# Wide attention of a fused two-layer transformer kernel: the query's scale moved into its evacuation, three-operand norms, the value projection ahead of the transposes, GpSimd's row sends two per step, and unrolled code

## The reference

```python
def _L1_xattn_ref(x, context, Wq, Wk, Wv, Wo, bo):     # 8 heads of 64
    scale = DIM_HEAD ** (-0.5)                          # 1/8
    q, k, v = heads(x @ Wq), heads(context @ Wk), heads(context @ Wv)
    attn = softmax(einsum('bhnd,bhmd->bhnm', q, k) * scale)
    return merge(einsum('bhnm,bhmd->bhnd', attn, v)) @ Wo + bo
x = x + _L1_xattn_ref(_layernorm(x), ctx_1024, ...)
x = x + _L1_ffn_ref(_layernorm(x), ...)                 # router: top 2 of 8 experts
```

## Time and profile before

| what | value |
|---|---|
| three runs | 1889.76, 1894.3, 1899.87 us, median 1894.3 |
| the profiled execution | 1891.22 us, its span 1889.4 us |
| busy share of the span | PE 79%, DVE 71%, ACT 62%, POOL 42% |
| wide attention: first to last group's exponentials | from 1144.9 to 1564.6 us of the span |
| its time for one step, mean of 64 | about 6.6 us |

### The profile page before, as it was taken

How to read it: one execution, slowest core, us unless ns; L and a number is a source line. 1 busy time by engine, 2 the same in 40 slices (tenths; PEclk the granted TensorE clock), 3 DMA queues, 4 the chain that set the end, 5 groups by cost and what they waited for, 6 DMA issues and landing times. The chain is left out here.

```text
span 1889.4 us, 62815 instructions
## 1 busy us (share of the span) xinstructions
PE 1485.4 (79%) x22193; PEld 1104.1 (58%) x22194; DVE 1343.5 (71%) x3761; ACT 1175.7 (62%) x2992; POOL 793.7 (42%) x836
## 2 busy tenths in 40 slices
PE   3999999838999889984329968888888885799990
PEld 2666666516666666663218845666666664678780
DVE  4888877648888888874536646788877875566675
ACT  2766666615555545544319957988877982677770
POOL 1000000033333333313755543456677766776661
PEclk9999999959999999996559977999999996899995
DMA  2222121001001001100122220011111101223228
GB/s 83 64 61 69 59 62 50 26 17 35 24 31 36 27 28 35 36 20 19 44 72 70 71 73 13 24 35 41 33 47 36 32 30 53 71 86 107 74 72 268
DMA packets 119875, 100.92 MB, mean 53 GB/s; under 512 B 18355, under 2 KB 111030, under 8 KB 119632
## 3 DMA queue, kind: packets, MB, share of 16 engines
q1 hardware_dynamic: 97712, 67.62, 12.3%
q0 software_dynamic: 12928, 25.60, 3.9%
q10 hardware_dynamic: 8992, 4.47, 0.8%
HBM read 43.30 MB, written 32.96 MB: 40 GB/s over the span
## 5 line engine op out<-in xcount | busy, mean ns | idle before, releaser
L2643 POOL DMA_INDIRECT e_back<-e_out_rows,e_G x142 | 151.6, 1067 | 72.0 <-issue 49.0
L1604 ACT ACTIVATE w_weights<-w_pS,w_ng 128x77 f32<-128x77 f32 x512 | 158.0, 340 | 25.9 <-DVE w_ng L1702 25.8
L580 ACT ACTIVATE m_PT<-m_pS 128x1024 f32<-128x1024 f32 x128 | 130.5, 1020 | 61.6 <-PE m_pS L450 59.8
L580 ACT ACTIVATE a_PT<-a_pS 77x1024 f32<-77x1024 f32 x128 | 130.6, 1020 | 48.4 <-PE a_pS L450 47.5
L731 DVE TENSOR_REDUCE m_mx<-m_pM 128x8 f32<-128x1024 f32 x128 | 155.4, 1214 | 3.1 <-PE m_pM L421 3.0
L1212 POOL DMA_INDIRECT e_rows<-re_R,re_index x128 | 129.2, 1009 | 62.6 <-issue 38.0
L2664 DVE TENSOR_TENSOR e_gl<-e_g,e_gh 128x512 f16<-128x512 f32 x142 | 98.3, 692 | 58.8 <-ACT e_g L2619 53.6
L851 POOL TENSOR_SCALAR a_var<-a_aggr 128x4 f32<-128x4 f32 x16 | 3.1, 194 | 291.4 <-DVE a_aggr L655 291.4
L1824 POOL TENSOR_TENSOR w_weights<-w_weights,w_rec 128x616 f32<-128x616 f32 x64 | 78.0, 1219 | 105.0 <-DVE w_rec L1706 104.7
L2616 ACT ACTIVATE e_gh<-e_pU 128x512 f16<-128x512 f32 x142 | 84.8, 598 | 46.9 <-PE e_pU L135 46.9
L1604 ACT ACTIVATION_READ_ACCUMULATOR w_weights<-w_pS,w_ng 128x1 f32 x512 | 113.7, 222 | 0.0
(11 more groups left out here) (401 smaller groups left out, 5661.1 us busy)
## 6 DMA issues: line engine op xcount, KB each, us to landing
e_G<-e_rows SPq DMA_DIRECT2D x106, 132.0 KB, 2.3
e_B<-e_back SPq DMA_DIRECT2D x16, 512.0 KB, 6.9
X<-in_x SPq DMA_DIRECT2D x16, 256.0 KB, 3.0
Qs<-a_qh SPq DMA_DIRECT2D x128, 32.0 KB
Qs<-m_qh SPq DMA_DIRECT2D x128, 32.0 KB
Ks<-m_kh SPq DMA_DIRECT2D x32, 128.0 KB
YW<-e_back SPq DMA_DIRECT2D x16, 256.0 KB, 3.1
w_stage<-in_late SPq DMA_DIRECT2D x16, 256.0 KB
```

Of the source, the lines that this page charges most:

```text
L580: act.activation(PT[:NK, b % 2, 8 * half:8 * half + 8, :], pS[:NK, :, :], ACT.Exp, scale=float(1.0 / np.sqrt(HD))).then_inc(exp_done, 1)
L1604: ac = act.activation(weights[:, b % 2, n, :], pS[:, n // HB, n % HB, :KC], ACT.Exp, bias=ng[:, b % 2, n:n + 1], scale=float(WD) ** -0.5, ...
L2643: pool.indirect_dma_start(out=back, out_offset=bass.IndirectOffsetOnAxis(ap=G[:, r, s, D:D + 1].bitcast(I32), axis=0), in_=out_rows[:, r, ...
```

## The change

All of it is in wide attention and in the router's `norm`:

- The query's parts hold -Q/8: ACT's copy gets scale -0.125, and DVE's low part becomes a `scalar_tensor_tensor`. The scores come out as -s/8, so the minimum over them is the exponentials' bias itself. The second DVE instruction of `take_max` and its semaphore go; the exponential's scale is -1.
- Both norms become `scalar_tensor_tensor` with three operands: the row, the mean as per-partition scalar, and the inverse deviation as a broadcast tensor.
- PE projects the values ahead of the transposes of the weights, and ACT copies them ahead of the weights.
- The sends go two per step in every step (in the last group three): of a pair's 16, four in the even group (b = 2, 3), eight in the odd one, four in the even group after it (b = 0, 1).
- POOL's `share` comes ahead of `roots`; `split_late` becomes `late_high` at b = 0 and `late_low` at b = 2.
- The loop is gone: all 16 groups are written out.

```diff
+Q_SCALE = -0.125
 ...
     def norm(self, dve, g):
         ...
-            dve.tensor_scalar(self.R[...], self.S[...], self.aggr[:, b, 0:1], self.rstd[:, b:b + 1], ALU.subtract,
-                              ALU.mult).then_inc(self.rows, 1)
+            dve.scalar_tensor_tensor(self.R[...], self.S[...], self.aggr[:, b, 0:1],
+                                     self.rstd[:, b:b + 1].rearrange("p (o n) -> p o n", o=1).to_broadcast([P, 1, D]),
+                                     ALU.subtract, ALU.mult).then_inc(self.rows, 1)
 ...
-            far, first, count = (4, 4 + 3 * b, 3) if g[1] % 2 else (3, 2 * b - 4, 2 if b > 1 else 0)
+            if g[0] is None and g[1] == NG - 1:
+                far, first, count = 4, 4 + 3 * b, 3
+            elif g[1] % 2:
+                far, first, count = 4, 4 + 2 * b, 2
+            else:
+                far, first, count = (3, 2 * b - 4, 2) if b > 1 else (5, 12 + 2 * b, 2)
 ...
         def walk(engine, begin, step, finish):
             begin()
-            groups(engine, lambda g, p, nxt, nxt2: [step(g, p, b, nxt, nxt2) for b in range(GB)], 4)
+            straight(engine, lambda g, p, nxt, nxt2: [step(g, p, b, nxt, nxt2) for b in range(GB)])
 ...
                     project("k", shift(g, 1), b)
+                project_values(g, b, nxt2)
                 if one:
                     turn_weights(*one)
-                project_values(g, b, nxt2)
 ...
-                    act.activation(Qh[:, p, b, :], pP[:, :TG], ACT.Copy).then_inc(hi_made, 1)
+                    act.activation(Qh[:, p, b, :], pP[:, :TG], ACT.Copy, scale=Q_SCALE).then_inc(hi_made, 1)
 ...
-                                        bias=ng[:, b % 2, n:n + 1], scale=float(WD) ** -0.5,
+                                        bias=ng[:, b % 2, n:n + 1], scale=-1.0,
 ...
+                keep_values(g, b)
                 if one:
                     keep_weights(*one)
-                keep_values(g, b)
 ...
-                    dve.tensor_tensor(Ql[:, p, b, :], pP[:, :TG], Qh[:, p, b, :], ALU.subtract).then_inc(evac, 1)
+                    dve.scalar_tensor_tensor(Ql[:, p, b, :], pP[:, :TG], Q_SCALE, Qh[:, p, b, :], ALU.mult,
+                                             ALU.subtract).then_inc(evac, 1)
 ...
-                dve.tensor_reduce(out=mx[:], in_=pS[:]..., op=ALU.max, axis=AX.X).then_inc(m_max, 1)
-                dve.wait_ge(m_max, lin(g, GB, b + 1))
-                dve.tensor_scalar(ng[:, b % 2], mx[:], -float(WD) ** -0.5, None, ALU.mult).then_inc(neg, 1)
+                dve.tensor_reduce(out=ng[:, b % 2], in_=pS[:]..., op=ALU.min, axis=AX.X).then_inc(neg, 1)
 ...
+                if one:
+                    share(*one)
                 if b == 3 and made:
                     route.roots(pool, made)
-                if one:
-                    share(*one)
 ...
                     route.send(pool, away, first, count)
+                if b == 0:
+                    late_high(g)
                 if b == 2:
-                    split_late(g)
+                    late_low(g)
```

More of the change, by code:

```diff
@@ L1104, in norm @@
         for b in range(GB):
-            dve.tensor_scalar(self.R[:, g[1] % 4, b:b + 1, 0, 0:D], self.S[:, bass.ds(lin(g, GB, b), 1), :],
-                              self.aggr[:, b, 0:1], self.rstd[:, b:b + 1], ALU.subtract,
-                              ALU.mult).then_inc(self.rows, 1)
+            dve.scalar_tensor_tensor(self.R[:, g[1] % 4, b:b + 1, 0, 0:D], self.S[:, bass.ds(lin(g, GB, b), 1), :],
+                                     self.aggr[:, b, 0:1],
+                                     self.rstd[:, b:b + 1].rearrange("p (o n) -> p o n", o=1).to_broadcast([P, 1, D]),
+                                     ALU.subtract, ALU.mult).then_inc(self.rows, 1)
     def lo(self, dve, g, bank, part):
@@ L1382, in wide_attention @@
         V = sb("V", [P, GB, WH_, WD], F32)
-        mx, ng = sb("mx", [P, WH_], F32), sb("ng", [P, 2, WH_], F32)
+        ng = sb("ng", [P, 2, WH_], F32)
         weights, sums, rec = sb("weights", [P, 2, WH_, KC], F32), sb("sums", [P, 2, WH_], F32), sb("rec", [P, 2, WH_], F32)
@@ L1396, in wide_attention @@
         v_ready, v_kept = sem("v_ready"), sem("v_kept")
-        s_ready, m_max, neg, exp_done = sem("s_ready"), sem("m_max"), sem("neg"), sem("exp_done")
+        s_ready, neg, exp_done = sem("s_ready"), sem("neg"), sem("exp_done")
         rec_done, shared, w_turned, w_kept = sem("rec_done"), sem("shared"), sem("w_turned"), sem("w_kept")
@@ L1682, in norm_rows @@
                 for b in range(start, start + count):
-                    dve.tensor_scalar(xn[:, b:b + 1, :], X[:, bass.ds(lin(g, GB, b), 1), :], aggr[:, b, 0:1],
-                                      rstd[:, b:b + 1], ALU.subtract, ALU.mult).then_inc(x_norm, 1)
+                    dve.scalar_tensor_tensor(xn[:, b:b + 1, :], X[:, bass.ds(lin(g, GB, b), 1), :], aggr[:, b, 0:1],
+                                             rstd[:, b:b + 1].rearrange("p (o n) -> p o n", o=1).to_broadcast([P, 1, D]),
+                                             ALU.subtract, ALU.mult).then_inc(x_norm, 1)
             def part(what, g, p, b):
@@ L1698, in take_max @@
                 dve.wait_ge(s_ready, lin(g, GB, b + 1))
-                dve.tensor_reduce(out=mx[:], in_=pS[:].rearrange("p o k t -> p (o k) t")[:, :, :KC], op=ALU.max,
-                                  axis=AX.X).then_inc(m_max, 1)
-                dve.wait_ge(m_max, lin(g, GB, b + 1))
-                dve.tensor_scalar(ng[:, b % 2], mx[:], -float(WD) ** -0.5, None, ALU.mult).then_inc(neg, 1)
+                dve.tensor_reduce(out=ng[:, b % 2], in_=pS[:].rearrange("p o k t -> p (o k) t")[:, :, :KC], op=ALU.min,
+                                  axis=AX.X).then_inc(neg, 1)
             def invert(g, b):
@@ L1810, in rows, with late_high @@
                 pool.tensor_tensor(rstd[:], var[:], c["mhalf"][:, 0:GB], ALU.pow).then_inc(ln_rstd, 1)
-            def split_late(g):
+            def late_high(g):
                 cols = bass.ds(lin(g, CL), CL)
@@ L1817, in split_late, with late_low @@
                                    ALU.add).then_inc(late_hi_done, 1)
+            def late_low(g):
+                cols = bass.ds(lin(g, CL), CL)
                 pool.wait_ge(late_hi_done, lin(g, 1, 1))
```

## The result

| | before | with the change |
|---|---|---|
| median | 1892.42 us (1889.76 to 1899.87, 4 runs) | 1846.77 us (1845.10 to 1851.03, 4 runs) |
| ratio | | 0.9744, 95% interval 0.9718 to 0.9771 |
| the profiled execution, its span | 1891.22, 1889.4 | 1851.03, 1849.2 |
| wide attention, X of group 0, b = 0 to X of group 15, b = 3 | 417.54 us | 372.54 us |

The forecast was 1852.0 with a range of 1836 to 1878; the median is 5.2 us under the forecast. The stage lost 45.0 us. The execution that was profiled lost 40.2, since the stages ahead of wide attention, whose code is the same, took 7.2 us longer in it (X of group 0 at 1152.10 instead of 1144.90), and what follows the stage 2.4 less.

What follows compares the result with a forecast made beforehand. Wide attention was taken as bound by ACT idling behind DVE work that POOL holds, worst at b = 3. Group savings of 26.2, 7.5, 4.6 and 1.2 us took 1891.2 to 1851.7, forecast as 1852.0 us, range 1836 to 1878.

Steps and rivals of the forecast that it cites:

- The sum: Wide attention: groups 4 to 11 -26.2 us, 12 to 14 -7.5, 0 to 3 -4.6, group 15 -1.2; together -39.5.
- The schedule of POOL: POOL's order, 47.9 us a pair: b = 3 norms free in even groups, 1.65 us late in odd ones.
- V ahead of the transposes: PE, ACT: values first end ACT's 0.34 us wait at b = 0, most of 0.86 at b = 2.
- The bias: DVE's bias instruction gone: 0.2 us at b = 3, its hold by POOL counted within ACT's 12.1 us wait.
- The norms: DVE's three-operand norms: no longer held by sends, still by `share`, `add` and late split; length ±0.2 us a group.
- The loop: PE's slow loop branch of 3.50 us, beside the held norm: unrolling keeps 2 us rather than gaining them.
- A: Norms held by POOL in even groups too: -22.5 us, about 1869 to 1870 us; chance 0.20.
- C: All three sets of norms in a group held by two POOL operations each: about 1930 us; chance 0.05.
- D: The stage stays held by POOL, whose order is merely rearranged: 1885 to 1897 us; chance 0.06.
- B: No norm held, POOL's 47.9 us a pair the bound in groups 4 to 11: 1846 us; chance 0.09.

Runs made afterwards that it cites:

- The first two versions above: The changed kernel with `add` at b = 0, or at b = 1, of odd groups, and `late_high` moved to b = 1 in groups 0 to 4: 1843.15 and 1841.19 us.
- the last version: The changed kernel with `add` at b = 1 of odd groups, moved `late_high`, and the norm ahead of `output_lo` on DVE: 1845.33 us.

## Why the prediction was right

**The sum.** By stage parts, forecast and measured: groups 4 to 11 -26.2 and -27.1; groups 12 to 14 -7.5 and -9.1; groups 0 to 3 -4.6 and -5.0; group 15 -1.2 and -3.8. Together -39.5 and -45.0. That the profiled execution (1851.03) fell on the forecast's 1851.7 is partly luck: the stage gave 5.5 us more than forecast, and the rest of this execution took 4.8 longer than in the one before. In groups 4 to 11 two mis-sized terms, below, cancel.

**The schedule of POOL held to 0.2 us.** It gave the start of `add` in even groups as 5.6 us after X of b = 3; it was 5.73 (1316.07 against 1310.34). For odd groups it gave 3.2 to 3.8 and 5.65 to 6.3 for the end of `share`; measured 3.97 and 6.42 (1288.17 and 1290.62 against 1284.20). I took 5.65, the early end, though nothing in a row spoke for it, and so put the odd b = 3 at 7.65 where it took 8.29: mis-sized by 0.64 at four steps. That `share` ahead of `roots` ends the wait for transposed weights was right too: it fell from 6.8 us to 0.3, and with the old order PE waits for `share` again and the stage takes 13.2 us more.

**V ahead of the transposes: right, sized too low.** The forecast was 6.34 at b = 0 and 5.9 at b = 2; the steps fell from 6.68 to 6.05 and from 6.84 to 5.87, and b = 1 by up to 0.29. Here a wait that was filled gave back more than its idle time: at b = 0 ACT was busy for 6.34 us of the old step and needs 6.05 for the new one. In groups 4 to 11, b = 0 and 1 gave 3.1 us more than forecast by the sums of their steps, and b = 3 2.5 less.

**The bias: right that it was held, wrong in what hung on it.** The step put 0.2 at b = 3 and left the rest inside the 12.1 us of waiting. In the kernel before it was held for 1.3 to 1.4 us at b = 2 of even groups, which cost those steps nothing (6.83 us, 6.84 in odd groups), and for 1.8 at b = 3 of groups 4 and 6. The 12.1 us did not fall with it: the wait is 14.2 now, 11.1 of it at the held norms of odd groups. Undone, the part costs 25.5 us in the stage, since the new order of GpSimd would hold the product for 2.35 to 2.65 us at b = 2 of even groups 4 to 10, and the norms of even groups behind it.

**The norms: this step failed.** I concluded from the earlier trace rows that "sends will no longer hold the norms" and saw in it what frees even groups. The row was true and beside the point. With the old form the stage is not longer, and in the kernel before the new form wins nothing. Even groups were free before as well, with the old form beside two sends (1.11 us in group 6), since `add` came after their norm then too; so the earlier trace rows did not show that sends hold `tensor_scalar`, and the 2.8 us that b = 3 of an even group won came from `share` and the bias product (2.3 of them are lost again with GpSimd's order undone, though the norms stay nearly free). The bounds on length were right: 1.13 us for four against 1.11. The Trainium skill's rule for the two forms ("VectorE: DVE Perf Modes", the perf-mode tier table), by which the estimate was 0.07 us lost per instruction, does not show here: their medians are 343 and 341 ns, and free steps at b = 3 differ by 0.02 to 0.03. The Trainium skill's rule on the lock ("SBUF — State Buffer", Who interferes with whom), that a DVE instruction with two SBUF inputs contends with a GpSimd one that reads SBUF, is what the held norms follow: 3.44 us for four beside `add` and `share`, 1.13 beside sends.

**`late_high` was not in the sum.** In groups 1 to 3, which have no sends, it now lies on the norm, and b = 3 takes 6.8 where the forecast had 6.0. From the timeline of the changed kernel, group 2:

```profile
1217.51 2.02 DVE L1106 SCALAR_TENSOR_TENSOR re_R<-X,re_aggr,re_rstd 128x128 f32<-128x128 f32 x4
1217.55 1.04 POOL L1823 TENSOR_TENSOR YW<-w_stage,zero 128x512 f16<-128x512 f32 x1
```

The first two versions above, which move it, take 5.98 there. I followed `late_high` only where it left (group 15), not where it went.

**The loop** was put at 2 us kept, on the ground that the norm would be free at the branch, though the forecast's own steps held it in odd groups. It is held there (group 7 is odd), so the branch would have stayed hidden: nothing either way.

**Rivals.** A (held everywhere), C (slower) and D (nothing changes) did not come; B's bound of 47.9 us a pair is close to the measured 48.7, and the last version runs a pair in 46.9, so that estimate of POOL's load was a little high.

## What to carry to other kernels

When two engines keep each other out, write down for each long operation of the one what lies beside it on the other, and at what distance, in every group form: here the price of the bias product and of the norms came from where `add`, `share` and the late split meet them, not from their form or length (an instruction on 8 elements a partition was held for up to 2.65 us). Look in both group forms of the trace before a wait is put down to one cause: a step like the held one stood there free. Test a part from both ends: two of the parts are worth nothing alone, and one of these 13 us together with the others. And where the code ahead of a stage makes executions differ by 12 us, compare the stage's own length in the trace.

## What the runs showed of the hardware that I had not expected

- A GpSimd tensor operation straight behind a send holds DVE's norms, the bias product and the ranking's operation with two SBUF inputs, the first of these from about 0.35 us before its recorded start. In the fourteen traces together, three-operand norms that would have ended up to 0.35 us ahead of it are held and those from 0.36 on free; of the old form those up to 0.37 are held (in the run with the bias alone) and those from 0.42 on free. Not every DVE operation is held: the batch-norm statistics, with one SBUF input, run beside `add` in 0.27 to 0.28 us (group 6 of the changed kernel, at 1316.89).
- The two forms do differ beside a send that another send follows: of the old form, an instruction that would end in the last 0.2 us of the send mostly waits for the send's end (in group 6 of the kernel before the second norm ended at 1321.57, the send at 1321.54), the three-operand form does not (1.13 for four beside two sends). It costs 0.2 us at most, and nothing here: four norms with such a wait still take 1.11.
